# Keys loaded in two parts, the third chunk's queries two slots sooner, and a preamble in another order

## The reference

```python
xn = _layernorm(x)                                  # x: 1 x 2048 x 512
q = (xn @ Wq)                                       # 16 heads x 32
k, v = split(xn @ Wkv)                              # 4 groups x 32
scores = einsum('brgtd,bgsd->brgts', q, k) / sqrt(32)
scores = where(causal, scores + bias, -inf)         # bias: slope of the head x distance
attn = softmax(scores); out = einsum('brgts,bgsd->brgtd', attn, v)
a = out @ Wo + bo
gate = xn @ Wg.T; up = xn @ Wu.T                    # Wg, Wu: 4096 x 512, decoded from 4 bits
f = (gelu(gate) * up) @ Wd.T                        # Wd: 512 x 4096
result = x + a + f
```

## Time and profile before

| | |
|---|---|
| median of 3 runs | 1660.21 us |
| the profiled execution, whole | 1660.44 us |
| its span in the profile | 1658.6 us |
| mean granted TensorE clock | 0.97 of full speed |
| busy share of the span | PE 86%, DVE 78%, POOL 60%, ACT 59% |
| main part begins | about 114 us into the span |

### The profile page before, as it was taken

The page is one execution under the profiler, slowest core; times in us unless marked ns, Lnnn a source line. Parts: engine busy times, 40 slices in busy tenths (PEclk is TensorE's granted clock), DMA queues, the critical chain, the costliest instruction groups (busy, mean ns, idle before and its releaser), DMA issues.

```text
span 1658.6 us, 28981 instructions
## 1 busy us (share of the span) xinstructions
PE 1434.5 (86%) x9281; PEld 687.2 (41%) x9281; DVE 1286.3 (78%) x2639; ACT 976.2 (59%) x2124; POOL 997.5 (60%) x670
## 2 busy tenths in 40 slices
PE   5977888989879898989879999889878999898598
PEld 4753443434434444434334434444434444343243
DVE  7755878787868888887858788888858787886475
ACT  3335656666646666566656666666656666665330
POOL 3225665766757666667656776666647676675340
PEclk9988999999989999999989999999989999999799
DMA  7777968888887889888887888788878879778666
GB/s 217 219 169 146 167 127 162 152 161 155 153 155 141 167 140 169 144 155 157 161 148 148 166 153 161 139 167 151 155 144 156 157 151 164 146 152 134 121 151 212
DMA packets 784367, 260.97 MB, mean 157 GB/s; under 512 B 734368, under 2 KB 755752, under 8 KB 783672
## 3 DMA queue, kind: packets, MB, share of 16 engines
q1 hardware_dynamic: 779896, 253.48, 80.0%
q10 hardware_dynamic: 4320, 5.64, 1.1%
HBM read 52.30 MB, written 21.89 MB: 45 GB/s over the span
## 4 chain that ended last, share of the span: by engine, by line
DVE 29%; PE 20%; issue 13%; ACT 10%; DMA 8%; POOL 7%; SPq 5%; ACTq 0%; DVEq 0%; POOLq 0%
PE up_ps L1325 6%; PE gate_ps L1325 5%; DVE mxp L1560 4%; ACT p L1447 4%; POOL pair L1706 4%; DMA pt<-pair 4%; DVE acc L1517 4%; PE down_ps L1303 4%; PE s_ps L1342 3%; DVE wf L380 3%; DVE dec L367 3%; ACT gl L1428 2%; DVE dec L371 2%; DVE prod L1541 2%; DVE s_ps L1562 2%
## 5 line engine op out<-in xcount | busy, mean ns | idle before, releaser
L1706 POOL TENSOR_TENSOR pair<-p,pair 128x1024 f16<-128x1024 f32 (+7 forms) x384 | 615.2, 1610 | 332.1 <-ACT pair L1457 329.2
L1447 ACT ACTIVATE p<-s_ps,shift 128x512 f32<-128x512 f32 (+3 forms) x640 | 393.2, 619 | 251.7 <-DVE shift L1581 250.0
L1342 PE MATMUL s_ps<-kst,qst 128*128 128x512 f32 (+3 forms) x640 | 344.3, 540 | 139.0 <-ACT p L1447 102.7
L1457 ACT ACTIVATE pair<-p 128x1024 f16<-128x1024 f32 (+7 forms) x384 | 308.2, 808 | 77.0 <-DMA pt<-pair 73.9
L1560 DVE TENSOR_REDUCE mxp<-s_ps 128x1 f32<-128x512 f32 x384 | 260.3, 683 | 94.8 <-PE s_ps L1342 92.7
L1714 POOL TENSOR_TENSOR il<-prod,ih 128x512 f16<-128x512 f32 x128 | 156.3, 1221 | 182.6 <-DVE ih L1549 182.6
L1342 PEld LDWEIGHTS s_ps<-kst,qst 128*128 128x128 f32 x640 | 123.4, 193 | 258.3 <-ACT p L1447 154.2
L1303 PE MATMUL down_ps<-wh,ih 128*128 128x512 f16 x506 | 196.6, 389 | 25.6 <-DVE acc L1517 25.6
L1303 PE MATMUL down_ps<-wh,il 128*128 128x512 f16 x506 | 193.9, 383 | 15.6 <-POOL il L1714 15.6
L1325 PE MATMUL up_ps<-xh,wh 128*128 128x512 f16 x512 | 200.0, 391 | 0.0
L1325 PE MATMUL gate_ps<-xh,wh 128*128 128x512 f16 x512 | 198.0, 387 | 0.6 <-DVE gl L1533 0.6
(11 more groups left out here) (249 smaller groups left out, 2055.6 us busy)
## 6 DMA issues: line engine op xcount, KB each, us to landing
o<-oraw SPq DMA_DIRECT2D x256, 64.0 KB, 2.0
qst<-q_parts SPq DMA_DIRECT2D x192, 64.0 KB
q_parts<-o SPq DMA_DIRECT2D x24, 256.0 KB, 3.3
pt<-pair SPq DMA_TRANSPOSE x384, 4.3
raw<-L_ffn_gate_W_packed_dram SPq DMA_DIRECT2D x16, 256.0 KB, 3.1
raw<-n_L_ffn_up_W_packed_dram SPq DMA_DIRECT2D x16, 256.0 KB, 3.1
raw<-L_ffn_down_W_packed_dram SPq DMA_DIRECT2D x32, 128.0 KB, 2.6
o<-l_recips SPq DMA_DIRECT2D x64, 64.0 KB, 2.1
```

Source lines behind the costliest of these rows:

```text
L1342: nc.tensor.matmul(s_ring[n % len(s_ring)][:, 0:cols], qst[:, c % 2, i4 * P:(i4 + 1) * P], kst[:, m * CH:m * CH + cols], start=True, stop= ...
L1447: nc.scalar.activation(p32[p % PR][:, at:at + cols], s_ring[n % len(s_ring)][:, 0:cols], ACT.Exp, bias=shift[t % len(shift)][:, 0:1], accu ...
L1457: nc.scalar.activation(pair[n % PH][:, 0:cols], p32[n % PR][:, 0:cols], ACT.Copy).then_inc(phi_done, 1)
L1706: nc.gpsimd.tensor_tensor(pair[n % PH][:, cols:2 * cols], p32[n % PR][:, 0:cols], pair[n % PH][:, 0:cols], ALU.subtract).then_inc(plo_done, 1)
```

## The change

Three things move; no arithmetic is added or taken away.

- **Keys in two parts.** `load_k` is called in slot 34 for columns 0 to 511, as soon as all but the last three blocks of the head before are done, and in slot 37 for the other 1536. The first block of the next head waits for the first part alone (`k_last`), block 5 (the first with m = 1, slot 45) for the rest.
- **Queries.** Chunk 2 is issued in slot 46 of the round before, for head 0 too, and `load_q` now stands directly behind the transposes of its slot.
- **Preamble.** `value_bound` goes behind the first projection on DVE, the low halves of chunk 0 between the two halves of chunk 1's norm, Wq's high part ahead of chunk 0's copies on ACT, the first `row_scales` from (1, 1) to (0, 4), the first `rows_hi` from (2, 4) to (3, 0). `first_head(1)` goes from (1, 2) to (1, 4), and SP's only `turn_rows` of the preamble to (3, 2), behind that slot's stores; the second weight's transposes go to the start of the main part. The values of chunk 3 are projected behind (3, 2) and finished behind (3, 3) instead of at the end.

```diff
-LOAD_Q_AT = {0: (0, 2), 6: (0, 3), 20: (1, 0), 37: (1, 1)}
-LOAD_K_AT, LOAD_V_AT = 37, 0
+LOAD_Q_AT = {46: (1, 2), 6: (0, 3), 20: (1, 0), 37: (1, 1)}
+LOAD_FIRST_Q_AT = 46
+LOAD_K_AT, LOAD_V_AT = (34, 37), 0
...
-SCALES_AT = {(1, 1): 0, (1, 4): 1, (2, 1): 2}
+SCALES_AT = {(0, 4): 0, (1, 4): 1, (2, 1): 2}
...
-ROWS_FIRST_AT = {(2, 4): 0, (3, 1): 1}
-TURN_FIRST_AT = {(3, 1): 0, (3, 3): 1}
+ROWS_FIRST_AT = {(3, 0): 0, (3, 1): 1}
+TURN_FIRST_AT = {(3, 2): 0}
+LAST_V = 2
...
-                def load_k(i):
-                    sp.wait_ge(block_done, i * NBLK)
+                def load_k(i, first):
+                    sp.wait_ge(block_done, i * NBLK - (NCH - 1 if first else 0))
+                    cols = slice(0, CH) if first else slice(CH, T)
                     for part, at in ((0, HD), (0, 2 * HD), (1, 3 * HD)):
-                        sp.dma_start(kst[at:at + HD, :].bitcast(F32), k_s[part, bass.ds(i // REP * HD, HD), :]
-                                     ).then_inc(k_in, 16)
+                        sp.dma_start(kst[at:at + HD, cols].bitcast(F32), k_s[part, bass.ds(i // REP * HD, HD), cols]
+                                     ).then_inc(k_last if first else k_in, 16)
...
-                turn_rows(sp, 2, 0, 0, acc[:, 2 * TPC + KT + 2, :].bitcast(F16))
+                for m in (1, 2):
+                    turn_rows(sp, m, 0, 0, acc[:, 2 * TPC + KT + m, :].bitcast(F16))
...
-                        if n == 0:
+                        if n == 0 and h % REP == 0:
+                            if h:
+                                pe.wait_ge(k_last, 48 + h // REP * 48)
+                            else:
+                                pe.wait_ge(k_in, K_FIRST)
+                        if h and h % REP == 0 and t == TPC and m == 1:
                             pe.wait_ge(k_in, K_FIRST + h // REP * 48)
```

More of the change, by code:

```diff
@@ L615, in _ @@
                             first_head(sp, 0)
+                        if (c, j) == (1, 4):
                             first_head(sp, 1)
@@ L730, in _ @@
                             turn_x(c + 1, k)
-                    project_v(c)
-                    if c == NCH - 1:
-                        pe.wait_ge(os_done, 1)
-                        pe.wait_ge(xl_done, KT * NCH)
-                        nc.tensor.transpose(turn[0][0:2 * KT, 0:P], oboth, ident[:]).then_inc(os_turned, 1)
-                        turn_v(c)
+                        if (c, j) == (NCH - 1, LAST_V):
+                            project_v(c)
+                        if (c, j) == (NCH - 1, LAST_V + 1):
+                            pe.wait_ge(os_done, 1)
+                            pe.wait_ge(xl_done, KT * NCH)
+                            nc.tensor.transpose(turn[0][0:2 * KT, 0:P], oboth, ident[:]).then_inc(os_turned, 1)
+                            turn_v(c)
+                    if c < NCH - 1:
+                        project_v(c)
             @block.scalar
@@ L760, in values_hi, with copy_v @@
                                          ACT.Copy, scale=vscale[:, 0:1]).then_inc(v_hi, 1)
+                def copy_v(c):
+                    act.wait_ge(v_sum, c + 1)
+                    if c >= 1:
+                        act.wait_ge(v_turned, c)
+                    nc.scalar.activation(vsum, vps[:], ACT.Copy).then_inc(vsum_done, 1)
                 root(0)
@@ L764, in _ @@
                 nc.scalar.activation(wkvs[0], wkv, ACT.Copy).then_inc(kv_hi, 1)
-                for k in range(KT):
-                    act.wait_ge(turned, k + 1)
-                    nc.scalar.activation(xt[0][0][:, k, :], first_ps[k][:], ACT.Copy).then_inc(xthi_done, 1)
                 act.wait_ge(wq_in, 16)
@@ L771, in _ @@
                 for k in range(KT):
+                    act.wait_ge(turned, k + 1)
+                    nc.scalar.activation(xt[0][0][:, k, :], first_ps[k][:], ACT.Copy).then_inc(xthi_done, 1)
+                for k in range(KT):
+                    if k == 2:
+                        root(1)
                     act.wait_ge(xtlo_done, k + 1)
                     nc.scalar.activation(xh[:, k, 0:CH], first_ps[k][:], ACT.Copy, scale=XS).then_inc(xh_done, 1)
-                root(1)
                 for c in range(NCH):
@@ L933, in _ @@
                                             ALU.subtract).then_inc(xtlo_done, 1)
-                value_bound()
-                layer_norm(1)
-                for k in range(KT):
-                    dve.wait_ge(xh_done, k + 1)
-                    nc.vector.scalar_tensor_tensor(xl[:, k, 0:CH], first_ps[k][:], XS, xh[:, k, 0:CH],
-                                                   ALU.mult, ALU.subtract).then_inc(xl_done, 1)
+                statistics(1)
+                for k in range(2):
+                    first_xl(k)
+                deviations(1)
+                for k in range(2, KT):
+                    first_xl(k)
                 for c in range(NCH):
@@ L948, in _ @@
                                                        ).then_inc(part_lo, 1)
+                        if (c, j) == (0, 0):
+                            value_bound()
                         if c and j == 0:
                             values_lo(c - 1)
+                        if (c, j) == (NCH - 1, LAST_V + 1):
+                            values_lo(c)
                         for k in TURN_X_AT[c > 0].get(j, ()) if c + 1 < NCH else ():
@@ L1185, in body @@
                             turn(h, p)
+                        if s in LOAD_Q_AT and i + LOAD_Q_AT[s][0] in range(HEADS) and (i >= 0 or s == LOAD_FIRST_Q_AT):
+                            load_q(i + LOAD_Q_AT[s][0], LOAD_Q_AT[s][1])
                         if i < 0 or s >= SLOTS:
@@ L1200, in body @@
                             spread_recips(sp, i - 1)
-                        for ahead, c in [LOAD_Q_AT[s]] if s in LOAD_Q_AT else ():
-                            if i + ahead < HEADS:
-                                load_q(i + ahead, c)
                         if i < LAST:
-                            if s == LOAD_K_AT and (i + 1) % REP == 0:
-                                load_k(i + 1)
+                            if s in LOAD_K_AT and (i + 1) % REP == 0:
+                                load_k(i + 1, s == LOAD_K_AT[0])
                             if s in TURN_ROWS_AT:
```

24 lines of the change are left out of this document (14 added, 10 removed).

## The result

The kernel with the change takes 1637.4 us (median of 4 runs, 1635.7 to 1641.0); the kernel before, run beside it, 1657.8. The ratio is 0.9878, with a 95% interval of 0.9845 to 0.991. The direction and the range held, but of the 34.8 us that were forecast only 20.4 came. The range, 1616 to 1643, had been drawn wide enough to take in rivals A and D; the time came out where rival A stood (1638), not at the forecast's 1626. So the range that held says little about the mechanism.

What follows compares the result with a forecast made beforehand. PE, busy 86% of the span, was taken as the bound, with its waits deciding; 24.2 (keys) + 2.2 (queries) + 0 + 8.4 (preamble) = 34.8 us off 1660.44, so 1626 us for the median, range 1616 to 1643.

Steps and rivals of the forecast that it cites:

- Rival A: Changes of keys: PE stops at block 5 for second keys or probabilities; 12 us gained instead of 24, 1638; chance 0.14.
- Rival D: Preamble: gain lost because DVE's and POOL's decoding sets its end whatever the order; 1634; chance 0.08.
- The keys: Three changes of keys: waits and slow matmuls behind them go; 24.2 us gained, between 19 and 25.7.
- Its first two steps: Changes of keys: first part lands 3.9 us before block 0 wants it; second part's waits at block 5 total 2.7 us.
- the last of the queries' paragraph: Heads with new values: load_v has 1.8 us more ahead of it, costing perhaps half a microsecond in each of three.
- its own sign for this: Heads with new keys: prediction is wrong if the three key waits go and these heads still take longer than others.
- The queries in head 0: Block 12 of head 0: load 4.8 us sooner, less 2.6 for two transposes ahead in SP's queue; net 2.2 us gained.
- The other heads: Queries in slot 46 delay the fourth transpose 1.8 us; nothing taken for it, 1.8 us per head as bad end.
- Rivals B and C: B: late fourth transpose costs 1.8 us in 15 heads, 1653, chance 0.08; C: slow clock too, 1687, chance 0.04.
- The sign named for B: Waits of PE for ACT over the run: more than 102.7 us would show that rival.
- The preamble: Start to main part: last preamble work ends at 105.3 instead of 113.7; 8.4 us gained, 4 to 11.
- the beginning: Start of preamble: new order leaves DVE without a gap; 0 taken, a gap opened or closed worth 2 us either way.

Runs made afterwards that it cites:

- e1_keys: Kernel before with the keys loaded in two parts and nothing else; 1644.97 us, ratio 0.9933.
- e4_no_values: Kernel with the change without the three later loads of values, so output differs from head 4 on; 1623.85 us, ratio 0.9806.
- e6_first_values: Kernel with the change, the first two tiles' values in buffers of their own, loaded in slot 22 of the round before; 1628.85 us, ratio 0.9829.
- e3_preamble: Kernel with the change, but keys and queries as before, leaving the preamble's order and the second weight's moved transposes; 1654.75 us, ratio 0.9982.
- e9_q_back: Kernel with the change, chunk 2's queries back in slot 0 for all heads but head 0; 1634.19 us, ratio 0.9858.
- e7_halves: Kernel with the change, the keys' first part 1024 columns instead of 512, issued in slot 35; 1641.97 us, ratio 0.9903.
- e12_q_then_store: Against e6_first_values: the store of a head's normalised outputs in slot 47 instead of 42, behind the queries; 1646.82 us, ratio 0.9944.
- e5_values_first: Kernel with the change, load_v in slot 46 of the round before, ahead of the queries and fourth transpose; 1632.03 us, ratio 0.9858.

## Why the prediction was right and wrong

**The keys, forecast 24.2, measured 9.5 in the profile (12.1 as the median of e1_keys).** Its first two steps held: the first part landed without a wait in all three heads (block 0 comes 8.09 to 8.10 us behind the last block, where it came 16.4 to 17.3 behind), and the waits for the second part sum to 3.2 us against the 2.7 forecast. The forecast took that part's landing as unchanged. By the medians it is not (3.3 us for its 192 KB, 4.1 for the whole), but PE waits for the last of three transfers, and at head 8 it goes on 5.67 us after the first was issued before (843.20 to 848.87) and 5.63 now (826.14 to 831.77). The step that failed is the last of the queries' paragraph: "`load_v` has the same 1.8 us ahead of it, but waits today for the last `values` of the head before; in three heads that may cost half a microsecond each". It costs 9.8 us of waits, and with the slow clock behind them and the load's own issues 14.4 us in the two rounds (e4_no_values, 13.5 between the medians); without the load the two rounds gain 23.9. About half of the 14.4 is shown to hang on the one buffer (e6_first_values gets back 7.4); the other 7.0 is not isolated.

The prediction had named its own sign for this: "I am wrong if the three waits for keys go and the heads with new keys still take longer than the others". That is what happened: the waits for keys fell from 24.8 to 3.2 us, and blocks 5 to 12 took 17.9 to 18.4 us at new keys against 13.6 in the other heads. By that sign the keys' term was wrong in its mechanism, whatever the total did.

Three things were not worked out in that step. First, the load's slack was never read: 6.15 us from the last `values` to the first, and 5 to 6 to land. Second, what stands ahead is the queries and the fourth transpose, 481.00 - 477.83 = 3.2 us, not 1.8. Third, SP was there in time before only because PE's 8 us of waiting let it catch up. The prediction said so of ACT's chain ("because the other engines caught up while PE stood still") and priced that at 2.0 us a head, but did not ask it of SP's own queue. e1_keys shows that no more than the keys' edit is needed: with the old place of the queries and of the transposes the waits for values are already 6.1 us.

**Rival A** had the kind of failure right ("the keys' wait only changes its name") and the time, 1638, near; its mechanism in the main was not: it put the wait on the second part of the keys (3.2 us in all) or on the probabilities. Those do come in, as the smaller part: around the three changes PE waits 5.2 us for them, 1.6 before. That its time came out near is luck. It had a chance of 0.14. The rule that would have raised it was in hand: a transfer that refills a buffer in place, on the queue that had its idle time taken, is late first.

**The queries in head 0, forecast net 2.2, measured 2.9** (blocks 5 to 12: 19.5 to 16.6 us). Both parts are seen apart: the two transposes cost 2.7 (e3_preamble, forecast 2.6), and the queries bring 22.2 - 16.6 = 5.6 (forecast 4.8). The wait at block 12 went whole instead of falling to 4 or 5 us. The load is issued at 121.76, 16.4 us behind block 0 where it was 18.2; that is 1.8 sooner, near the net 2.2. But PE also comes to block 12 later, because it waits longer for ACT just before (4.24 us ahead of the blocks at 121.75, against 1.05 in the profile before): it is there at 125.58, 20.3 us behind block 0, where it was at 137.73 - 6.90 = 130.83, 16.3 behind. The forecast held PE's own time fixed, and so had a wait left over; the sum came out near because both ends moved, which is luck.

**The other heads, forecast 0, measured 0** (e9_q_back), apart from `load_v`. Rivals B and C are out. The sign named for B, more than 102.7 us of waits for ACT, did show (106.9), but it was no good sign: e3_preamble, with the queries at their old place, has 106.8, and e7_halves, with them at the new one, 102.6.

**The preamble, forecast 8.4, measured 9.2** in this profile. The chain that ends it is the one forecast, and its end at 104.5 stands against 105.3. PE's two waits of the earlier trace rows, 3.53 and 1.90 us, are gone, and the last projection ends at 100.6 (forecast 101.4). In the eleven profiles of kernels with this preamble (this one and the experiments but for e1_keys) the first block starts between 102.8 and 108.1, in the mean at 106.0; that is 8.3 us under the 114.3 of the two with the old order. Five are late (107.3 to 108.1) and six early (102.8 to 105.3). In the late ones PE waits longer, 2.0 to 3.4 us, for a copy of DVE about 46 us in (0.4 to 0.8 in the early ones). The traces show what holds DVE up. It scales a chunk in four instructions (`deviations`) of some 0.54 us each, and with the new order POOL starts copies of its own (L657, L662) before these are through. A late one, e3_preamble, and the early kernel with the change:

```profile
39.92 5.21 DVE L858 TENSOR_SCALAR acc<-acc 128x512 f32<-128x512 f32 x4
```

```profile
39.76 2.57 DVE L859 TENSOR_SCALAR acc<-acc 128x512 f32<-128x512 f32 x4
```

In all five late profiles one of the four takes 3.2 us, about as long as POOL's first five copies beside it, which take 0.61 to 0.66 us each. In the six early ones none of the four takes over 1.0, and POOL's first copy takes 0.73 to 0.92. In the two profiles with the old order POOL starts only during the last of the four, and all keep 0.54. So the beginning, which the prediction put at 0, holds a loss of 2 to 3 us in five of the eleven profiles. That rests on the traces alone; no run moves POOL's copies, and what decides which way it goes stays open.

As a median of runs e3_preamble shows less, 2.3 us (0.2 to 5.8) where 8.3 less 2.7 would be 5.6; that is within its interval. Rival D is out.

**The sum.** Of 34.8 us forecast, 14.7 are missing in the keys' term, 0.7 and 0.8 came on top in the other two, and 2.9 went in the other rounds and behind the last block, within what profiles differ: 34.8 - 14.7 + 1.5 - 2.9 = 18.7, against 19.4 in the spans; the rest is head 0 behind block 12 (0.7). The chance of 0.92 for faster was justified. The best version, e6_first_values, is 8.5 us under the kernel with the change and ends at 1629; against its own runs of the kernel before it brings 29.0 of the 34.8 us.

## What to carry to other kernels

When a wait of the pacing engine is removed, the in-order queues lose the idle time in which they caught up. List every transfer issued in the next few microseconds and write beside each when its buffer is freed, what stands ahead of it in the queue, how long it takes to land and when it is first read. A single buffer that is refilled in place had the least slack here, and double-buffering only its first tiles was enough to take its wait away, and half of the loss with it. And a wait that shrinks by tens of microseconds proves nothing until one has looked for what grew beside it: in e12_q_then_store ACT's 35 us moved one instruction on.

## What the runs showed of the hardware

- The issue of DMAs is not small beside the transfers. In the 3.2 us before `load_v` at head 4 SP did four plain issues in 1.72 us and one transpose in 1.24, while the transfer itself was there 3.27 us after the end of its own issue (486.33 - 481.00 - 2.06). The Trainium skill, page "DMA: Bandwidth & Descriptors", section "Issuing engines are not separate DMA queues", says that using several engines to start DMAs only saves the sequencer's time for it, "which is usually small relative to the DMA itself". Here this time was the difference between no wait and 3.57 us: in e5_values_first, with the load ahead of the queries and the fourth transpose, there is none.
- VectorE and GpSimd can hold each other up. Beside GpSimd's copies about 40 us in, one of VectorE's scalings (128x512, float32) took 3.18 to 3.25 us in five profiles, and the longest one 0.85 to 0.97 in six others; the first of the four, with nothing of GpSimd's beside it, takes 0.55.
- How far PE's clock falls behind a wait does not follow from the wait's length alone. Behind the 3.57 us at the values of head 4 the granted clock is 0.50. Behind 2.00 us for the second keys in e4_no_values it is 0.53 (first row below), behind 2.36 us at the same place in e9_q_back it is 1.00 (second row), and behind 1.97 us for the values there 0.60 (third row); each is a mean over the row's stretch. This is one reason why 9.8 us of waits could cost more than themselves, and why the cost of one wait can't be read from its length.

The window of e4_no_values:

```profile
472.00:475.60 3.60, 3.60 (x10) 1.43 (x11) 0.67 (x4) 0.99 (x2) 0.39 (x1) 0.53 1.23 237
```

And two windows of e9_q_back:

```profile
470.20:474.00 3.80, 3.80 (x18) 1.77 (x18) 0.72 (x5) 1.14 (x2) 0.62 (x1) 1.00 1.25 235
...
485.40:489.40 4.00, 4.00 (x18) 1.58 (x18) 1.44 (x3) 2.50 (x5) 1.82 (x1) 0.60 0.68 137
```
